# The first load of a pairwise-product kernel: half of the partitions of sixteen fields, ahead of W

## The reference

```python
vid = jnp.einsum('bfd,de->bfe', x, W)
idx_i, idx_j = jnp.triu_indices(F_, k=1)      # F_ = 32: 496 pairs
y = x[:, idx_i, :] * vid[:, idx_j, :]         # 4096 x 496 x 64
```

## Time and profile before

| what | value |
|---|---|
| median of 3 runs | 1284.25 us |
| profiled execution, its time on the device | 1283.99 us |
| its span, first to last instruction | 1282.7 us |
| DMA, moved in the span | 553.73 MB, mean 432 GB/s |
| VectorE busy | 1077.8 us (84%) |
| TensorE busy | 166.0 us (13%) |

### The profile page before, as it was taken

The page is one execution under the profiler, slowest core; times in us unless marked ns, Lnnn a source line. Parts: engine busy times, 40 slices in busy tenths (PEclk is TensorE's granted clock), DMA queues, the critical chain, the costliest instruction groups (busy, mean ns, idle before and its releaser), DMA issues. The chain is left out here.

```text
span 1282.7 us, 1107 instructions
## 1 busy us (share of the span) xinstructions
PE 166.0 (13%) x256; PEld 65.1 (5%) x256; DVE 1077.8 (84%) x255; POOL 0.2 (0%) x4
## 2 busy tenths in 40 slices
PE   2030110303010020030301203002020020302000
PEld 1010000101000000010100001001000000101000
DVE  6799998989889647889999979918899898999582
POOL 0000000000000000000000000000000000000000
PEclk8565565656556556575655556556555565657555
DMA  9999999999999999999999999999999999999999
GB/s 391 433 439 435 429 437 442 429 425 441 441 425 431 439 429 433 425 446 437 425 435 443 429 425 441 436 422 433 426 431 446 429 427 446 435 427 425 448 433 394
DMA packets 10370, 553.73 MB, mean 432 GB/s; under 512 B 1152, under 2 KB 1152, under 8 KB 1152
## 3 DMA queue, kind: packets, MB, share of 16 engines
q1 hardware_dynamic: 9216, 508.56, 91.6%
q10 hardware_dynamic: 1152, 45.15, 8.3%
HBM read 33.62 MB, written 520.09 MB: 432 GB/s over the span
## 5 line engine op out<-in xcount | busy, mean ns | idle before, releaser
L194 DVE TENSOR_TENSOR mem<-mem,vid 128x2048 f32<-128x2048 f32 (+13 forms) x255 | 1077.8, 4296 | 181.6 <-DMA out_dram<-mem 151.7
L255 PE MATMUL vid<-mem 128*128 (+1 forms) x256 | 166.0, 811 | 1010.6 <-PEq L254 1010.6
L255 PEld LDWEIGHTS vid<-mem 128*128 128x128 f32 x256 | 65.1, 267 | 1110.6 <-issue 1110.6
L362 POOL MEMSET const-bfloat16-1.0<- 128x1 bf16 x1 | 0.1, 103 | 0.0
L362 POOL MEMSET const-uint8-127<- 128x1 uint8 x1 | 0.1, 102 | 0.0
L362 POOL MEMSET const-float32-0.0<- 128x1 f32 x1 | 0.1, 100 | 0.2 <-issue 0.2
L362 POOL MEMSET const-float32-1.0<- 128x1 f32 x1 | 0.1, 99 | 0.0
## 6 DMA issues: line engine op xcount, KB each, us to landing
out_dram<-mem SPq DMA_DIRECT2D x7, 7168.0 KB, 21.0
out_dram<-mem SPq DMA_DIRECT2D x4, 6144.0 KB, 20.9
mem<-in_r_x_dram SPq DMA_DIRECT2D x2, 7936.0 KB, 38.7
mem<-in_r_x_dram ACTq DMA_DIRECT2D x1, 7936.0 KB, 25.9
out_dram<-mem ACTq DMA_DIRECT2D x1, 7168.0 KB, 37.9
mem<-in_r_x_dram SPq DMA_DIRECT2D x2, 2304.0 KB, 44.0
mem<-in_r_x_dram ACTq DMA_DIRECT2D x1, 2304.0 KB, 36.9
mem<-in_L_rec_W_x_dram ACTq DMA_DIRECT2D x1, 1088.0 KB, 5.6
```

The costliest lines, as they stand in the source:

```text
L194: self.engine.tensor_tensor(*operands, MULT).then_inc(self.dve, 1)
L255: nc.tensor.matmul(vid[:, b * BANK : b * BANK + BANK, :], lhsT=w, rhs=mem[:, bass.ds(k * step + (first + b * BANK), BANK), :], start=True, ...
L362: nc = _bacc.Bacc("TRN2", target_bir_lowering=False, num_devices=1, dynamic_dma_scratch_size=256)
```

## The change

A new load, named `early`, becomes the first DMA of ScalarE's queue. It loads partitions 0 to 63 of the sixteen units of `h0`. `x0` follows as before. What was `h0` is then loaded in its place for partitions 64 to 127 alone (`h00`), and `h1` and `h2` (now `h10` and `h20`) follow as before. A field can now have two loads, so `loaded` holds a list for each, and ScalarE waits for every semaphore of that list before it adds one to `go` for a half tile. All of the bytes, addresses and everything behind the first loads are the same; there are 73 DMAs for 72.

```diff
 HEAD = range(6), [(16, 16), (286, 124), (410, 36)]
+EARLY_RUN = 0
+FIRST, OTHERS = slice(0, P // 2), [slice(P // 2, P)]
...
         for t, f in fields:
-            loaded[t, f] = s
+            loaded.setdefault((t, f), []).append(s)
         return s
...
+    lo, n = HEAD[1][EARLY_RUN]
+    at = sum(m for _, m in HEAD[1][:EARLY_RUN])
+    load(act, mem[FIRST, lo : lo + n, :], x[FIRST, at : at + n, :], "early", fields(HEAD[0], lo, n))
     ws = load(act, whole[:, : 1 + HALF, :], x0[:, : 1 + HALF, :], "x0", [(0, f) for f in range(HALF)])
...
-    def stretch(q, tiles, runs, name):
+    def stretch(q, tiles, runs, name, run=None):
...
-            made.append(load(q, mem[:, lo : lo + n, :], x[:, at : at + n, :], f"{name}{r}", fields(tiles, lo, n)))
+            for i, rows in enumerate(OTHERS if r == run else [slice(0, P)]):
+                made.append(load(q, mem[rows, lo : lo + n, :], x[rows, at : at + n, :], f"{name}{r}{i}", fields(tiles, lo, n)))
...
-    stretch(act, *HEAD, "h")
+    stretch(act, *HEAD, "h", EARLY_RUN)
...
-            for s in [ws, *(loaded[t, b * BANK + f] for b in half for f in range(BANK))]:
+            for s in [ws, *(s for b in half for f in range(BANK) for s in loaded[t, b * BANK + f])]:
                 act.after(s)
```

## The result

| kernel | median, us | runs | against before |
|---|---|---|---|
| before | 1284.12 (1283.75 to 1284.92) | 22 | |
| changed | 1286.22 (1285.52 to 1286.92) | 22 | +2.10 us, ratio 1.0016, 95% interval 1.001 to 1.0022 |

The changed kernel is 2.1 us slower, 0.16%: inside the 0.2% bound of the prediction, but its fastest run is slower than the slowest of before. The profiled execution took 1286.08 us, with a span of 1284.8 (before 1283.99 and 1282.7).

The account below looks back on a forecast made before the run. The prediction took the DMA to bound the kernel, with VectorE following. Issues 0, early +1.21, h00 +1.21, ramp -0.5, VectorE 0 and meeting 0 gave +1.9 us on 1284.25: 1286.1 us, range 1283.8 to 1287.1.

Parts of the forecast that it names:

- the 0.2% bound: Whole kernel: about 0.2% (2.57 us) is what a measurement can tell from no change; chance of staying within, 0.86.
- A transfer of 64 partitions runs at half speed: Early and h00 at the start: half of the ways into SBUF, so each takes 2.42 us, 1.21 more.
- as fast as any: Rival, early and h00: 64 partitions run at full speed, giving 1284.0 us (1283.7 to 1284.4); chance 0.27.
- The issues cost nothing: Front of ScalarE's queue: one more issue, 0.38 to 0.45 us, is covered by early's transfer; 0 us.
- The ramp hides a part: DMA's start, 1 to 4 us: the ramp hides 0.5 us of early's extra 1.21.
- VectorE starts late and that is free: VectorE's start: 1.2 to 2.4 us later, hidden by its first wait of 4.05 us for slot 0; 0 us.
- Loads and stores meet as before: 25 to 34 us, first store among loads: the existing 1.2 us loss stays; 0, between -0.3 and +0.3.
- rival of a worse meeting: 27 to 35 us: nothing hidden in the ramp and the 1.2 us loss grows; 1286.8 to 1287.9 us; chance 0.11.
- What the DMA loses comes out at the end: Whole kernel: a microsecond in which the DMA moves nothing, wherever it lies, comes out at the end.

Follow-up runs that it names:

- order alone: Against the changed kernel: all 128 partitions of h0 loaded as one transfer ahead of x0, nothing left for h00; 1283.63 us, 0.57 under before.
- late VectorE: The kernel before, loads unchanged, but TensorE's first matmul also waits for h0, so VectorE starts at 12.30; 1284.10 us, 0.26 under before.
- before again: The kernel before, unaltered, run once more for a second profile; no separate time is given.
- changed again: The changed kernel, unaltered, run once more for a second profile; 1286.28 us, +2.03 against before.
- order alone again: The kernel with all of h0 as one transfer ahead of x0, run once more; 1283.72 us, 0.53 under before.
- two queues: Against the changed kernel: h0 ahead of x0, partitions 0 to 63 from SyncE's queue, 64 to 127 from ScalarE's; 1286.25 us, +1.89 against before.
- that of the middle partitions: Against the changed kernel: early is partitions 32 to 95, then 0 to 31 and 96 to 127 behind x0; 1284.98 us, +0.78 against before.
- The kernel cut by fields: Against the changed kernel: early is eight of h0's sixteen fields over all 128 partitions, the other eight behind x0; 1284.24 us, +0.04 against before.
- split alone: Against the changed kernel: x0 stays first, then h0 as partitions 0 to 63 and 64 to 127; 1285.80 us, +1.6 against before.

## Why the prediction was right, and where steps of it were not

The forecast was 1286.1 in a range of 1283.8 to 1287.1; 1286.22 was measured, +2.10 where +1.9 was forecast. The mechanism that it rested on, the half speed, is shown. That the sum came out within 0.2 us is luck: the start cost 0.7 more than the +1.9, the tail another 0.6, and a stall that went away gave 1.2 back.

- *A transfer of 64 partitions runs at half speed* (+1.21 twice, taken against "as fast as any"). Right. From x0's landing to that of h00 it is 2.44 us on the mean for 0.524 MB, 215 GB/s. Cut by fields it costs nothing, partitions 32 to 95 run at full speed, and for a store it costs the same. The argument by which I took it, that loads and stores run alike, was weak: both readings fit it. What carried it was the likelihood of a limit on the partitions' side, and only the experiments show it. The Trainium skill's page "SBUF — State Buffer", section "Door 1: The DMA port swizzle", which the forecast named, has the rule, and its 218 GB/s agrees with 197 to 221 in the windows that hold packets of a half alone.
- *The issues cost nothing* (0). Wrong by 0.3 us. The issue of early takes 0.54 us, not 0.38 to 0.45, and the first packet begins at 2.06 in place of 1.75: nothing moves from 1 to 2 us. It was so in each kernel whose first transfer has 64 partitions (first packets from 2.06 to 2.12), and in none whose first has 128 (1.73 to 1.76).
- *The ramp hides a part* (-0.5). Wrong: of the 1.21 about 0.1 was hidden. x0 lands 2.63 later on the mean; less the late start of 0.32 and early's own 1.21, 1.10 are left. In the second execution 1.58 are left, so nothing was hidden there. With the late start and nothing much hidden, x0 landed at 8.9, outside the forecast's 7.6 to 8.2. With the late start the loss of the start is +2.6, where the sum had +1.9; this is above the +2.5 that I had for its end.
- *VectorE starts late and that is free* (0). Right: 2.6 late, its wait shrunk by 1.65, and with VectorE held back alone the time doesn't rise. But the wait that the forecast gave, about 2.4 plus what the DMA is late, would be some 4.3 with its +1.9; 2.40 was measured, as slot 0 landed only 0.98 late.
- *Loads and stores meet as before* (0, between -0.3 and +0.3). Wrong, by more than its bounds: -1.15. The forecast saw the loss of 1.2 us in the windows and took it to go with the meeting itself. It is a stall that before has and that goes away when the work behind the loads starts 2 us later, or when the loads do. The changed kernel has both and loses nothing there. My rival of a worse meeting was wrong in its sign.
- *What the DMA loses comes out at the end.* Right, with an addition that I had not. VectorE waits for the last of 16 counts, and the DMA engines drift apart: in the changed kernel the spread is 0.5 us at slot 0 and 1.8 at slot 58 (1.2 in before). VectorE's last eight products wait for slot 59's last count, so they start 1.93 late though the DMA is 1.34 late on the mean, and in the tail, where the DMA has hardly any work queued (slot 61 lands at 1244.5 on the mean, slot 62 is issued at 1244.1), the others stand idle for it: the last +0.6. By terms: +0.32 (late start) + 2.27 (two halves) - 1.17 (no stall, h1 to slot 0) - 0.08 (slots 0 to 58) + 0.59 (tail) = +1.93, the profiled difference at slot 63.

The changed kernel keeps this gain, while order alone and the late VectorE lose most of theirs between slots 20 and 23. The packets show where: a second stall lies where the loads of tiles 6 to 10 come in, the first of their packets near 453 us. From 430 to 465 us I added up what each packet took over its usual length (2.42 us for a store's of 64 KB, 2.34 for a load's of 62), over 16 engines:

```
                  stall, us     step of the mean landing
                                from slot 20 to 23, us
before            0.29          0
before again      0.59          +0.37
changed           0.12          -0.15
changed again     0.17          -0.13
order alone       0.96          +0.74
order alone again 0.95          +0.72
late VectorE      1.13          +1.05
two queues        1.05          +0.80
```

Less before's 0.29 the stall is the step, to about 0.2 us. So some 0.15 us of the changed kernel's result is again a stall of which it has less than before. Which kernels meet it, and why, isn't shown.

Still open: what makes h2's packets stall. It isn't how far h2 has come: 38 of its packets had begun at the store's issue in before, with the stall, and 40 in the changed kernel, 44 in that of the middle partitions, without it. The kernel cut by fields, with an issue at 28.3, has a stall of 0.98 us; all with an issue at 29.6 or later have at most 0.04, but split alone has none either with an issue at 27.6, when h1 is still under way.

## What to carry to other kernels

When a kernel is bound by its DMA, look at which partitions each transfer covers, and not only at its bytes: on this chip a transfer of partitions 0 to 63 or 64 to 127 moves at half speed, so cut a load by columns (+0.04 us here, nothing that can be told from 0) and not by partitions. A stall of the trace belongs to a moment as much as to an operation: an edit that shifts things by 2 us may remove it, so let the forecast's bounds take in its whole size on both sides. And compare two traces by a mean over the DMA engines as well as by the last one, or the drift between them passes for an effect.

## What the hardware showed that I had not expected

- A first transfer of 64 partitions takes 0.54 to 0.58 us to issue, with the first packet at 2.06 to 2.12 us; one of 128 partitions takes 0.38 to 0.39, with the first packet at 1.73 to 1.76.
- Packets of 8 KB into partitions 32 to 95 take 0.31 us, as they do in a transfer of all 128 (an estimated 424 GB/s over 16 engines, worked out from the 0.31); into 0 to 63 or 64 to 127 alone they take 0.60 to 0.63, and loads of a half move 197 to 221 GB/s. A store of 64 partitions moves 204 to 210.
- Two transfers on two queues, issued in the same 0.01 us: the second queue's first packet begins 1.85 us after the first's, and the two transfers land one after the other.
- With the first store issued at 27.7 to 27.8 us, load packets that begin in the next 5 us or so take up to 2.4, 2.8 and 3.4 times their length in three executions, 1.2 to 1.4 us in all; with all the work behind the loads 2 us later they don't. A second such stall lies near 453 us, of 0.1 to 1.1 us, where loads come in among stores.
- The 16 engines' spread at a landing goes from 0.5 to 1.8 us within one execution of the changed kernel with the same work for each; in before it is 1.2 at both slots, 0 and 58.
